# Cross-attention over 12544 keys: the keys' low part taken at another place in Vector's order

## The chip, the cores and the metric

The kernel runs on one core of a Trainium2 chip. The metric is the device time of one execution in microseconds; lower is better. The core has a matrix engine (TensorE, PE in the rows; PEld is its weight load), Vector (DVE), Scalar (ACT), GpSimd (POOL) and SyncE (SP), which here issues all transfers. Each engine works through its own list of instructions in order, and they meet only at semaphores.

## The reference

The reference is four layers on a state x of 128 rows and 256 columns. Each layer adds a cross-attention over a context of 12544 rows, then a self-attention, then a feed-forward block, each from a layer norm of x. The change touches the cross-attention of layers 0, 2 and 3. Layer 3's is, in short:

```python
q = _split_heads(query @ Wq + bq)          # 16 heads of 16
k = _split_heads(key @ Wk + bk)            # key = value = the context, 12544 x 256
v = _split_heads(value @ Wv + bv)
logits = jnp.einsum('bhqd,bhkd->bhqk', q, k) / jnp.sqrt(jnp.float32(DH))
logits = logits + mask * -1000000000.0
attn = jax.nn.softmax(logits, axis=-1)
out = jnp.einsum('bhqk,bhkd->bhqd', attn, v)
return out @ Wo + bo
```

Layer 0 has a mask and no Wo, layer 2 no mask.

## The kernel before, in words

`cross_attention_turned` (called for the stages L0x, L2x and L3x) goes through the keys in 14 blocks of 896 (`NB`, `KB2`), with a running maximum per query and head. A block has 16 waves; a wave g handles two heads and one half of the block (448 keys for the maxima). Every operand of an exact product is split into a high part, rounded to the matrix engine's format, and a low part, the difference.

In each wave PE makes two maximum products (L904, `maxima`), each into one of three banks `m_bank`; Vector reduces each to one column of `tops` (L1132, `top_of`) and so frees the bank. The product at place n of the ring waits for the one at place n - 3: the second product of wave g + 1 waits for the first maximum of wave g, and the first product of wave g + 2 for the second maximum of wave g. Seven waves later (`LAG`) PE makes the scores of the same wave (L915, `scores`), Scalar takes their exponentials (L1037), and every other wave PE multiplies them with the values (L940).

After four waves a group of heads has its maxima. At g % 4 == 0 Vector takes the highest of the three columns (L1146, `raise_top`) and splits it into two columns of `nat`: a cast (L1156) and a subtract (L1158), `split_top`. In wave g + 1 PE turns these (L927, `turn_q`), after it has waited for the split, and Scalar copies the result into `q_sub`.

Beside this the next block is projected. In the odd waves PE runs `project_next`: items 0 to 3 in waves 1, 3, 5 and 7 are the keys (L877), items 4 to 7 in waves 9 to 15 the values (L882). All items share one bank, `p_proj`. For a key item Scalar writes the high part with the bias (L1021, `evacuate`) and Vector the low part (L1093, `k_low`), in the even wave that follows: item i in wave 2i + 2. The next item waits on PE until the bank has been read (`k_split` counts the low parts):

```python
if i <= 4:
    e.wait_ge(sem("k_split"), 4 * b + i)
```

PE's order in a wave is maxima, scores, values, project_next, turn_q.

SyncE waits for the fourth low part of a block, then issues 24 transfers that stack the keys (L763), and behind them the load of the context for the block after next (L745). POOL (`split_ctx`) waits for that load, casts it (L833) and subtracts (L835) into `ctx_part`. It then works on the running maximum and scales the accumulator once a block (L854, after Scalar has made alpha in wave 4).

Vector's order in a wave, written out by hand at L1168 to L1182, was: first maximum, raise, second maximum, split, accumulate, k_low.

Of the kernel before, what the change touches and what calls it, by code (L numbers as in the profile page):

```python
# [23 lines left out]
class Module:  # L24
# [8 lines left out]
    def ps(self, name, shape=(P, 512), dtype=F32):  # L33
        return self.stack.enter_context(self.nc.psum_tensor(f"{self.name}_{name}", list(shape), dtype))

    def sem(self, name):

        if name not in self.sems:
            self.sems[name] = self.nc.alloc_semaphore(f"{self.name}_{name}")
        return self.sems[name]  # L40
# [597 lines left out]
NB = NKEYS // KB2  # L638
QUADS = 4
SLOTS = 8  # L640
WAVES = 16
# [9 lines left out]
def cross_attention_turned(nc, st, name, w, mask_kind):  # L651
# [53 lines left out]
    p_proj, p_oT = ps("p_proj"), ps("p_oT")  # L705
# [7 lines left out]
    def m_at(g, i):  # L713
        k = g % WAVES
        return g // WAVES * M_BLOCK + 2 * k + i + (k > 11)
    m_o_at = lambda b: (b + 1) * M_BLOCK + M_O
    def m_done(n):
        return (n + 1 - (n >= M_O) if n < NB * M_BLOCK else NB * M_BLOCK - (n < NB * M_BLOCK + M_O))
# [14 lines left out]
    with nc.Block() as block:  # L733

        @block.sync
        def _(e):
# [10 lines left out]
            def stack(b):  # L747
                odd = b % 2

                if b >= 2:  # L750
                    e.wait_ge(sem("s_made"), s_done(s_at((b - 2) * WAVES + 15, 1)))
                if mask_kind:
                    for r in range(2):
                        at = GROUP * r + MASK
                        e.dma_start(k_stack[at:at + 2, odd].bitcast(F32),
                                    mask_dram[:, b * KB2:(b + 1) * KB2].bitcast(F32).unsqueeze(1).broadcast_to([2, SLOTS, KB2])
                                    ).then_inc(sem(f"mask_stacked_{odd}"), 16)
                e.wait_ge(sem("k_split"), b * 4 + 4)
                for j in range(QUADS):
                    for r in range(2):  # L760
                        for n, (_, part) in enumerate(PRODUCTS):
                            at, of = GROUP * r + HD * n, HD * (2 * j + r)
                            e.dma_start(k_stack[at:at + HD, odd, j::4, :].bitcast(F32),  # L763
                                        kT[of:of + HD, odd, part].bitcast(F32)).then_inc(sem(f"k_stacked_{odd}_{j}"), 16)
# [323 lines left out]
        def _(e):  # L1088

            def k_low(b, i, bank):  # L1090
                part, keys = i // 2, slice(i % 2 * HALF, (i % 2 + 1) * HALF)
                e.wait_ge(sem("k_high"), 4 * b + i + 1)
                e.scalar_tensor_tensor(kT[:, b % 2, LOW, part, keys], bank[:, 0:HALF], bias_k[:, part:part + 1],  # L1093
                                       kT[:, b % 2, HIGH, part, keys].bitcast(F32), ALU.add, ALU.subtract).then_inc(sem("k_split"), 1)
# [33 lines left out]
            def top_of(g, r):  # L1128
                b, half = g // WAVES, g % 4 // 2
                n, h = m_at(g, r), g // 4 % 4 * 4 + g % 2 * 2 + r  # L1130
                e.wait_ge(sem("m_made"), m_done(n))
                e.tensor_reduce(tops[:, b % 2, h, half:half + 1], m_bank[n % RING][:, 0:HALF], AX,  # L1132
                                ALU.max).then_inc(sem("m_free"), 1)
# [3 lines left out]
            def raise_top(q):  # L1137
                b, h = q // 4, q % 4 * 4
                e.wait_ge(sem("m_free"), m_done(m_at(4 * q + 3, 1)))
                if b:  # L1140
                    e.wait_ge(sem("kept"), b)
                else:
                    e.wait_ge(sem("tops_set"), 1)
                if b >= 2:
                    e.wait_ge(sem("stepped"), b - 1)
                e.tensor_reduce(top[:, b % 2, h:h + 4], tops[:, b % 2, h:h + 4, :], AX, ALU.max).then_inc(sem("raised"), 1)  # L1146

            def split_top(q):
                b, h = q // 4, q % 4 * 4
                t = top[:, b % 2, h:h + 4].rearrange("q (p r) -> q p r", p=2)  # L1150
                if b:
                    e.wait_ge(sem("s_made"), s_done(s_q_at(q - 4)))
                else:
                    e.wait_ge(sem("q_max_made"), 2)
                e.wait_ge(sem("raised"), 3 * q + 1)
                e.tensor_copy(columns(q, HIGH).bitcast(F32R), t).then_inc(sem("raised"), 1)  # L1156
                e.wait_ge(sem("raised"), 3 * q + 2)
                e.tensor_tensor(columns(q, LOW).bitcast(F32R), t, columns(q, HIGH), ALU.subtract).then_inc(sem("raised"), 1)  # L1158

            def accumulate(b):  # L1160
                n = m_o_at(b)
                e.wait_ge(sem("m_made"), m_done(n))
                e.wait_ge(sem("scaled"), b + 1)
                a = acc[:, :, 0:HD + 1]
                e.tensor_tensor(a, a, m_bank[n % RING][:].rearrange("p (h d) -> p h d", h=HX)[:, :, 0:HD + 1],
                                ALU.add).then_inc(sem("m_free"), 1)

            for g in range(LAST_G):  # L1168
                u = g - LAG
                if g < WAVE_END:  # L1170
                    top_of(g, 0)
                if g % 4 == 0 and 0 < g <= WAVE_END:
                    raise_top(g // 4 - 1)
                if g < WAVE_END:
                    top_of(g, 1)
                if g % 4 == 0 and 0 < g <= WAVE_END:
                    split_top(g // 4 - 1)
                if u % WAVES == 4 and u > 4:
                    accumulate(u // WAVES - 1)

                if g % 2 == 0 and g // WAVES + 1 < NB and 0 < g % WAVES <= 8:
                    k_low(g // WAVES + 1, g % WAVES // 2 - 1, p_proj)  # L1182

            e.wait_ge(sem("m_free"), m_done(m_o_at(NB - 1)))
            e.reciprocal(rsum[:], acc[:, :, HD]).then_inc(sem("rsum"), 1)
# [1373 lines left out]
```

## Time and profile before

| | us |
|---|---|
| three runs, median (lowest to highest) | 2619.21 (2602.45 to 2624.37) |
| the profiled execution | 2617.17 |
| its span, first to last instruction | 2615.4 |
| L0x, L2x, L3x, blocks 1 to 12 together | 1213.35 |
| mean granted TensorE clock | 0.914 |

The span is that of the profiled execution; around it lie 1.8 us. In the rows, a start is counted from the span's first instruction, and a block starts with its first maximum product. The profile has one more large stage, L1x (another function), and the small layers between.

### The profile page before, as it was taken

How to read it: one execution, taken by the hardware profiler on the slowest of the kernel's cores; microseconds unless marked ns; L12 is line 12 of the kernel's file. 1: busy time of each engine (PE TensorE's matmuls, PEld its weight loads, DVE VectorE, ACT ScalarE, POOL GpSimd, SP SyncE). 2: the span in 40 equal slices, each digit the busy share in tenths (PEclk: the TensorE clock that was granted, in tenths of full speed). 3: DMA queues.
4: the chain of work that ended last, by engine and by line, in shares of the span. 5: the costliest groups of instructions: out<-in, count | busy, mean ns of one | idle time of the engine just before them, and what ended most of it. 6: DMA issues, size and time to landing. Idle time of an engine off the chain costs nothing. (4 is left out here: it accounts for less than half of the span.)

```text
span 2615.4 us, 67791 instructions
## 1 busy us (share of the span) xinstructions
PE 2300.0 (88%) x26351; PEld 1866.4 (71%) x26351; DVE 1703.0 (65%) x4076; ACT 1482.2 (57%) x2965; POOL 405.9 (16%) x345
## 2 busy tenths in 40 slices
PE   6999999877999999996666999999955999999958
PEld 4788888675777777775535778877743888788738
DVE  4666666527888888886724666676725666666632
ACT  2666666625777777774023666666621666666621
POOL 3221112002211221210001122222001122222000
PEclk7999999989999999997577899999956899999959
DMA  5666666365444344332044766666514666666525
GB/s 119 111 116 118 117 118 104 47 208 148 108 120 105 99 117 120 94 83 55 1 134 80 121 113 107 112 107 107 77 46 91 123 112 113 110 114 116 74 82 201
DMA packets 149181, 277.48 MB, mean 106 GB/s; under 512 B 31599, under 2 KB 69312, under 8 KB 148941
## 3 DMA queue, kind: packets, MB, share of 16 engines
q1 hardware_dynamic: 148942, 274.13, 51.2%
q8 instruction: 171, 2.80, 0.4%
q14 instruction: 68, 0.56, 0.1%
HBM read 118.86 MB, written 0.33 MB: 46 GB/s over the span
## 5 line engine op out<-in xcount | busy, mean ns | idle before, releaser
L1132 DVE TENSOR_REDUCE L3x_tops<-L3x_m_bank 128x1 f32<-128x448 f32 x448 | 262.0, 619 | 156.8 <-PE L3x_m_bank L904 154.8
L1132 DVE TENSOR_REDUCE L0x_tops<-L0x_m_bank 128x1 f32<-128x448 f32 x448 | 262.0, 619 | 154.8 <-PE L0x_m_bank L904 152.7
L1132 DVE TENSOR_REDUCE L2x_tops<-L2x_m_bank 128x1 f32<-128x448 f32 x448 | 262.0, 619 | 148.8 <-PE L2x_m_bank L904 146.7
L454 ACT ACTIVATE L1x_prob<-L1x_p_s,L1x_neg_max 128x512 f32<-128x512 f32 (+1 forms) x400 | 275.8, 689 | 117.8 <-DVE L1x_neg_max L565 115.1
L560 DVE CUSTOM_DVE_ANT_0 L1x_p_s<-L1x_p_s,L1x_mask 128x512 f32<-128x512 f32 (+1 forms) x400 | 273.7, 684 | 35.8 <-PE L1x_p_s L320 30.5
L1037 ACT ACTIVATE L2x_prob<-L2x_s_bank 128x512 f32<-128x512 f32 x448 | 219.5, 542 | 92.0 <-PE L2x_s_bank L915 90.8
L1037 ACT ACTIVATE L3x_prob<-L3x_s_bank 128x512 f32<-128x512 f32 x448 | 219.5, 542 | 91.9 <-PE L3x_s_bank L915 90.8
L1037 ACT ACTIVATE L0x_prob<-L0x_s_bank 128x512 f32<-128x512 f32 x448 | 219.5, 542 | 90.4 <-PE L0x_s_bank L915 89.2
L329 PE MATMUL L1x_p_t<-net_ident,L1x_prob 128*128 128x128 f32 x1568 | 239.0, 273 | 10.6 <-ACT L1x_probT L175 10.5
L329 PEld LDWEIGHTS L1x_p_t<-net_ident,L1x_prob 128*128 128x128 f32 x1568 | 192.1, 140 | 48.8 <-ACT L1x_probT L175 13.6
L320 PE MATMUL L1x_p_s<-L1x_k_stack,L1x_q_stack 96*128 96x512 f32 (+1 forms) x400 | 182.2, 457 | 1.9 <-DVE L1x_q_stack L544 1.9
L175 ACT COPY L1x_probT<-L1x_p_t 128x512 f32<-128x512 f32 (+1 forms) x300 | 173.1, 577 | 5.1 <-PE L1x_p_t L329 5.1
L915 PEld LDWEIGHTS L3x_s_bank<-L3x_q_sub,L3x_k_stack 52*128 52x128 f32 x1568 | 124.2, 191 | 9.8 <-ACT L3x_prob L1037 6.6
L915 PEld LDWEIGHTS L2x_s_bank<-L2x_q_sub,L2x_k_stack 50*128 50x128 f32 x1568 | 123.8, 190 | 9.6 <-ACT L2x_prob L1037 6.3
L915 PEld LDWEIGHTS L0x_s_bank<-L0x_q_sub,L0x_k_stack 52*128 52x128 f32 x1568 | 122.8, 189 | 9.4 <-ACT L0x_prob L1037 6.1
L346 PE MATMUL L1x_p_oT<-L1x_probT,L1x_v 128*32 128x128 f32 x3136 | 126.9, 279 | 0.5 <-ACT L1x_probT L175 0.5
L915 PE MATMUL L3x_s_bank<-L3x_q_sub,L3x_k_stack 52*128 52x128 f32 x1568 | 116.9, 262 | 3.1 <-ACT L3x_prob L1037 2.9
L915 PE MATMUL L2x_s_bank<-L2x_q_sub,L2x_k_stack 50*128 50x128 f32 x1568 | 116.7, 262 | 3.1 <-ACT L2x_prob L1037 2.9
L904 PE MATMUL L0x_m_bank<-L0x_k_stack,L0x_q_max 52*128 52x448 f32 x448 | 111.9, 479 | 8.2 <-DMA L0x_k_stack<-L0x_kT 6.7
L904 PE MATMUL L3x_m_bank<-L3x_k_stack,L3x_q_max 52*128 52x448 f32 x448 | 112.2, 481 | 7.9 <-DMA L3x_k_stack<-L3x_kT 6.4
L915 PE MATMUL L0x_s_bank<-L0x_q_sub,L0x_k_stack 52*128 52x128 f32 x1568 | 115.5, 260 | 3.1 <-ACT L0x_prob L1037 2.9
L904 PE MATMUL L2x_m_bank<-L2x_k_stack,L2x_q_max 50*128 50x448 f32 x448 | 110.4, 476 | 4.4 <-DMA L2x_k_stack<-L2x_kT 2.5
(724 smaller groups left out, 4524.0 us busy)
## 6 DMA issues: line engine op xcount, KB each, us to landing
L0x_k_stack<-L0x_kT SPq DMA_DIRECT2D x336, 112.0 KB, 4.0
L2x_k_stack<-L2x_kT SPq DMA_DIRECT2D x336, 112.0 KB, 4.0
L3x_k_stack<-L3x_kT SPq DMA_DIRECT2D x336, 112.0 KB, 4.0
L1x_k_stack<-L1x_kT SPq DMA_DIRECT2D x288, 128.0 KB, 2.4
L3f_w<-in_L_ffn_w SPq DMA_DIRECT2D x16, 1024.0 KB, 9.2
L0x_ctx<-in_ctxT SPq DMA_DIRECT2D x14, 896.0 KB
L2x_ctx<-in_ctxT SPq DMA_DIRECT2D x14, 896.0 KB
L3x_ctx<-in_ctxT SPq DMA_DIRECT2D x14, 896.0 KB
```

The costliest lines, as they stand in the source:

```text
L175: copy(probT[:, h % PT_RING, 0:nk], p_t[h % T_RING][:, 0:nk]).then_inc(sem(copied(h)), 1)
L320: e.matmul(p_s[h % S_RING][:, 0:nk], q_stack[0:ROWS, h, :], k_stack[0:ROWS, odd, h // 2, 0:nk], start=True, stop=True).then_inc(sem("score ...
L329: i = e.transpose(p_t[h % T_RING][:, t * P:(t + 1) * P], prob[:, h % P_RING, t * P:(t + 1) * P], ident[:])
L346: i = e.matmul(p_oT[VW * s:VW * s + VW, g * P:(g + 1) * P], v[:, odd, t, h, :], probT[:, h % PT_RING, t * P:(t + 1) * P], start=t == 0, st ...
L454: e.activation(prob[:, h % P_RING, 0:nk], p_s[h % S_RING][:, 0:nk], ACT.Exp, bias=neg_max[:, odd, h:h + 1]).then_inc(sem("exped"), 1)
L560: e.tensor_tensor_reduce(s, s, mask[:, odd, 0:nk], 1.0, -3e38, ALU.add, ALU.max, block_max[:, h:h + 1]).then_inc(sem("head_maxed"), 1)
L904: e.matmul(m_bank[n % RING][:, 0:HALF], q_max[rows_of(r), slot_of(g), :], k_stack[rows_of(r), b % 2, slot_of(g), half * HALF:(half + 1) * ...
L915: mm = e.matmul(s_bank[s_at(u, r) % RING][:, at * P:(at + 1) * P], k_stack[rows_of(r), b % 2, slot_of(u), t * P:(t + 1) * P], q_sub[rows_o ...
L1037: e.activation(prob[:, k % 3, u % 2 * 2 + r, 0:nt, :].rearrange("p t n -> p (t n)"), s_bank[n % RING][:, 0:nt * P], ACT.Exp).then_inc(sem( ...
L1132: e.tensor_reduce(tops[:, b % 2, h, half:half + 1], m_bank[n % RING][:, 0:HALF], AX, ALU.max).then_inc(sem("m_free"), 1)
```

## The change

In Vector's loop the low part is taken directly behind the first maximum of an even wave. Before, it came last in the wave. The waits and counts of all instructions are the same.

```diff
                 if g < WAVE_END:
                     top_of(g, 0)
+
+                if g % 2 == 0 and g // WAVES + 1 < NB and 0 < g % WAVES <= 8:
+                    k_low(g // WAVES + 1, g % WAVES // 2 - 1, p_proj)
                 if g % 4 == 0 and 0 < g <= WAVE_END:
                     raise_top(g // 4 - 1)
                 if g < WAVE_END:
...
                     split_top(g // 4 - 1)
                 if u % WAVES == 4 and u > 4:
                     accumulate(u // WAVES - 1)
-
-                if g % 2 == 0 and g // WAVES + 1 < NB and 0 < g % WAVES <= 8:
-                    k_low(g // WAVES + 1, g % WAVES // 2 - 1, p_proj)
```

So the order becomes: first maximum, k_low, raise, second maximum, split. In waves 2 and 6 there is no raise and no split; in waves 4 and 8 there are both.

## Rows read from the trace of the kernel before

**Rows 1.** The page, part 1: busy time, share of the span, instructions.

```profile
PE 2300.0 (88%) x26351; PEld 1866.4 (71%) x26351; DVE 1703.0 (65%) x4076; ACT 1482.2 (57%) x2965; POOL 405.9 (16%) x345
```

**Rows 2.** Windows: blocks 1 to 12 of L0x, L2x, L3x; columns in the first line.

```profile
core 0: us, PE busy (x) PEld busy (x) DVE busy (x) ACT busy (x) POOL busy (x), PEclk, DMA share, GB/s
75.12:478.58 403.46, 387.71 (x5354) 325.95 (x5353) 274.29 (x588) 262.97 (x553) 75.25 (x58) 0.99 0.65 112
1465.29:1870.85 405.56, 387.66 (x5354) 325.70 (x5353) 276.42 (x588) 262.98 (x553) 75.19 (x58) 0.99 0.64 108
2052.40:2456.73 404.33, 388.97 (x5354) 327.32 (x5353) 273.91 (x588) 262.97 (x553) 75.27 (x58) 0.98 0.65 112
```

**Rows 3.** PE's waits in L0x, all blocks: us in total, times, longest.

```profile
PE L0x_p_proj L882 <- DVE L0x_kT L1093: 15.9, 13, 4.0
PE L0x_p_proj L877 <- DVE L0x_kT L1093: 5.2, 15, 0.7
```

**Rows 4.** Windows of three single blocks of L0x, columns as in rows 2.

```profile
280.01:312.60 32.59, 31.94 (x448) 26.85 (x447) 22.19 (x49) 21.92 (x47) 6.75 (x5) 1.00 0.64 111
176.49:212.30 35.81, 33.47 (x448) 28.18 (x447) 23.88 (x49) 21.91 (x47) 6.73 (x5) 0.95 0.69 116
345.70:379.45 33.75, 31.95 (x447) 26.85 (x446) 23.34 (x49) 21.92 (x47) 6.74 (x5) 1.00 0.65 115
```

**Rows 5.** Timeline of PE, block from 280.01: start, us, instruction [idle before <-releaser].

```profile
290.50 1.48 PE L877 MATMUL L0x_p_proj<-L0x_ctx_part,L0x_wk_part 128*128 128x448 f32 x6 [0.32 <-DVE L0x_kT L1093]
...
297.65 0.47 PE L904 MATMUL L0x_m_bank<-L0x_k_stack,L0x_q_max 52*128 52x448 f32 x2
...
298.73 1.70 PE L882 MATMUL L0x_p_proj<-L0x_wv_part,L0x_ctx_part 128*128 128x256 f32 x12 [0.33 <-DVE L0x_kT L1093]
300.27 0.38 PE L927 MATMUL L0x_s_bank<-net_ident,L0x_nat 128*128 128x128 f32 x2
300.58 0.47 PE L904 MATMUL L0x_m_bank<-L0x_k_stack,L0x_q_max 52*128 52x448 f32 x2
...
306.67 0.47 PE L904 MATMUL L0x_m_bank<-L0x_k_stack,L0x_q_max 52*128 52x448 f32 x2
...
309.20 0.48 PE L904 MATMUL L0x_m_bank<-L0x_k_stack,L0x_q_max 52*128 52x448 f32 x2
```

**Rows 6.** Timelines of Vector and Scalar, waves 6 to 9 of that block.

```profile
293.72 0.68 DVE L1093 SCALAR_TENSOR_TENSOR L0x_kT<-L0x_p_proj,L0x_bias_k,L0x_kT 128x448 fp32r<-128x448 f32 x1
...
296.57 0.62 DVE L1132 TENSOR_REDUCE L0x_tops<-L0x_m_bank 128x1 f32<-128x448 f32 x1 [1.07 <-PE L0x_m_bank L904]
...
297.71 0.17 DVE L1156 CAST L0x_nat<-L0x_top 128x4 fp32r<-128x4 f32 x1
...
298.00 0.68 DVE L1093 SCALAR_TENSOR_TENSOR L0x_kT<-L0x_p_proj,L0x_bias_k,L0x_kT 128x448 fp32r<-128x448 f32 x1
298.59 1.15 DVE L1132 TENSOR_REDUCE L0x_tops<-L0x_m_bank 128x1 f32<-128x448 f32 x2
...
296.18 0.63 ACT L1021 ACTIVATE L0x_kT<-L0x_p_proj,L0x_bias_k 128x448 fp32r<-128x448 f32 x1 [0.35 <-PE L0x_p_proj L877]
```

**Rows 7.** Timeline of POOL: the split's subtract L835, the scaling L854.

```profile
89.44 4.03 POOL L835 TENSOR_TENSOR L0x_ctx_part<-L0x_ctx,L0x_ctx_part 128x1792 fp32r<-128x1792 f32 x1
...
254.84 0.66 POOL L854 TENSOR_TENSOR L0x_acc<-L0x_acc,L0x_alpha 128x272 f32<-128x272 f32 x1 [7.54 <-ACT L0x_alpha L1049]
...
292.93 4.03 POOL L835 TENSOR_TENSOR L0x_ctx_part<-L0x_ctx,L0x_ctx_part 128x1792 fp32r<-128x1792 f32 x1
...
2405.36 4.03 POOL L835 TENSOR_TENSOR L3x_ctx_part<-L3x_ctx,L3x_ctx_part 128x1792 fp32r<-128x1792 f32 x1
```

**Rows 8.** Timeline of Vector: casts and low parts of other blocks.

```profile
58.95 0.68 DVE L1093 SCALAR_TENSOR_TENSOR L0x_kT<-L0x_p_proj,L0x_bias_k,L0x_kT 128x448 fp32r<-128x448 f32 x1
...
92.78 0.71 DVE L1156 CAST L0x_nat<-L0x_top 128x4 fp32r<-128x4 f32 x1
...
253.18 0.62 DVE L1132 TENSOR_REDUCE L0x_tops<-L0x_m_bank 128x1 f32<-128x448 f32 x1 [1.08 <-PE L0x_m_bank L904]
...
2376.62 0.68 DVE L1093 SCALAR_TENSOR_TENSOR L3x_kT<-L3x_p_proj,L3x_bias_k,L3x_kT 128x448 fp32r<-128x448 f32 x1
```

## Prediction, made before the changed kernel was run

> **What bounds the kernel now.** I read the page first, then the windows of the stages, the waits on TensorE (PE), single blocks, and the timeline of the waves that the change touches. The page has PE busy for 88% of the span [rows 1]. The change sits in the function that stages L0x, L2x and L3x call; blocks 1 to 12 of them fill 1213.35 us, 36 blocks of 33.70 us on average, with PE busy 96% of that and its granted clock at 0.98 to 0.99 [rows 2]. PE sets the pace. What PE waits for is nearly always k_low (L1093 on Vector, DVE): in L0x 15.9 us ahead of the value projection L882 and 5.2 us ahead of the key projection L877 [rows 3].
>
> These waits are of two kinds. The short one is in every block. In wave 5 PE stands 0.32 us for k_low before L877, in wave 9 0.33 us before L882; wave 9 lasts 300.58 - 297.65 = 2.93 us, while wave 13, with the same work and no k_low, lasts 309.20 - 306.67 = 2.53 [rows 5]. So the wait costs 0.40 a wave, and this block of 32.59 us is otherwise without a gap worth naming: PE is busy for 31.94 of it [rows 4].
>
> The long one comes from GpSimd (POOL). The split's cast L1156 takes 0.17 us when undisturbed [rows 6], but in one block it starts at 92.78, in the middle of POOL's subtract L835 (89.44 to 93.47), and ends at 93.49 [rows 7, 8]. In block 0 k_low starts only at 58.95 for that reason, and PE waits 4.0 us [rows 3, 8]. Whenever the cast of wave 8 meets L835, it stands until L835 is over, and k_low stands behind it in Vector's queue, with PE waiting. Two stretched blocks show the price: one lasts 33.75 at full clock, the other 35.81 at clock 0.95 with PE busy 33.47 instead of 31.94, 1.53 us more for the same work [rows 4]. Over the 36 blocks the excess above the undisturbed 32.59 is 1213.35 - 36 x 32.59 = 40.1 us.
>
> **The change, step by step.** Nothing is added or taken away; four k_low a block move ahead, in waves 2 and 6 past one maximum (0.61 us), in waves 4 and 8 past raise, maximum, cast and subtract as well. No wait value changes.
>
> *What goes from PE.* In wave 8 the first maximum starts at 296.57 and is over by 297.19; k_low starts now at 298.00 [rows 6], then at about 297.13, and ends at 297.81 instead of 298.68. PE could begin L882 0.40 earlier than 298.73, at 298.33 [rows 5], so k_low is there 0.5 in advance and the whole 0.40 goes. The same holds for wave 4 with wave 5. In waves 2 and 6 PE doesn't wait for k_low, so that move brings nothing: 0. Saved: 2 x 0.40 x 36 = 29 us. An undisturbed block then lasts 31.79.
>
> *Does k_low then wait itself?* It needs ScalarE's high part, L1021, which ends at 296.18 + 0.63 = 296.81, 0.38 before the first maximum ends [rows 6]. Cost 0; both come from the same PE stream, so an earlier projection moves both.
>
> *What the second maximum's delay costs.* It frees its bank some 0.7 us later (about 298.4, or 298.0 once wave 5's saving is counted). The next to use that bank is the first maximum product of wave 10, at 300.58 - 0.80 = 299.78 [rows 5]. Cost 0, with 1.7 us in hand. Vector's total for the wave is the same, so wave 9's maxima start where they do now (298.59 [rows 6]).
>
> *The collision with L835.* It doesn't go: the cast now starts about 0.55 us behind the end of k_low. SyncE issues the next stack of keys behind k_low of wave 8, then the context load, and POOL's cast and subtract follow the load. From that k_low's end to the end of the next L835 it takes X: 93.47 - 59.63 = 33.84 us in the first case, 2409.39 - 2377.30 = 32.09 in the last of 33 [rows 7, 8]; over all 33 the least is 31.7, the mean 32.9, the most 34.3. The cast is then held for X - 31.79 - 0.55, some 0.6 us on average and 2.0 at most. What is behind it now? Not k_low, but PE's transpose L927 (it wants the split) and wave 9's maxima. L927 comes at 300.27 - 0.80 = 299.47 [rows 5], behind a projection that PE can do meanwhile, and the split would be ready near 298.3: 1.15 us of cover. The first maximum of wave 9 would end near 298.9, wanted at 299.9: about 0.95 us of cover. Held times above 0.95 occur in 8 of the 33 cases and sum to 3.2 us for 36 blocks; with 1.53 us for a lower clock once, 5 us remain of the 40. The ends of this cost are 0 (all covered) and 36 x 0.6 = 22 us, if nothing is covered; I take 5, since a 1.5 us projection is queued ahead of L927.
>
> *A second meeting.* In wave 4 the cast moves by 0.6 us, to about 254.95 (the first maximum starts at 253.18 [rows 8]), and there it meets POOL's L854, 254.84 to 255.50 [rows 7]. It would be held 0.55 us in each block. The maxima of wave 5 then end 0.3 us before they are wanted. Cost 0; uncovered it would be 36 x 0.55 = 20 us.
>
> *Is k_low itself held by POOL?* k_low of wave 6 starts at 293.72 and takes 0.68 us, inside an L835 that runs from 292.93 to 296.96 [rows 6, 7]. So it isn't, and it needs no cover. The Trainium skill says otherwise for some forms ("SBUF — State Buffer", section "SBUF: two separate sides"): one pair of ports is an exclusive lock between GpSimd and a Vector instruction that runs in a two-port mode or has two SBUF inputs, for the whole instruction. k_low reads keys and a bias column from SBUF beside its bank; counted as two, it would stand behind L835 like the cast. The trace decides against that count, and agrees with the rule on the cast.
>
> *Block 0.* PE waits more there: in L0x 5.2 - 12 x 0.32 = 1.4 us before L877 and 4.0 before L882 [rows 3], where L927 still comes behind the held cast, so that about the projection's 1.7 to 2.5 us are won. That makes about 4 us in L0x; I put 2 each on L2x and L3x, whose waits were shorter. 8 us, between 3 and 12.
>
> *SyncE and the stack.* k_low of wave 8 ends 1.3 us earlier, 0.4 of it from wave 5; the 24 issues start earlier with it, and their data is wanted one block on. Nothing waits for them now in blocks 1 to 12, and nothing will. 0.
>
> **The sum.** 2617.17 (the profiled execution, span 2615.4) - 29 - (40 - 5) - 8 = 2545 us. The median of the runs shown is 2619.21, 2 us above the profiled one, within their spread of 22 us; I keep 2545.
>
> **Rivals.**
> 1. *Less cover.* The held cast (0.6 a block), wave 5's lateness and clock losses reach PE after all, because L927 or the maxima turn out to be wanted earlier. For: the cover of wave 5 is only 0.3 us. Against: in a wave PE always has scores and a projection between. 22 us instead of 5, and 5 for wave 5: 2567.
> 2. *k_low is held by POOL* at its new place, with a later phase of L835. Then the long waits stay and only wave 5's 0.40 x 36 = 14 us go, with 3 in block 0: 2600. Against: the 0.68 us above. The lock rule of the Trainium skill's SBUF page is the one that would bring it about.
> 3. *The change doesn't do what it says*, since the ring of k_low, stack, load and L835 sets the block's length anyway. For: X is 32.9, close to the mean block of 33.70. Against: blocks of 32.59 exist. Time: 2617.
> 4. *Slower: a collision in every block.* Now a stretched block often puts the next one out of L835's way. With k_low ahead of the cast that relief is gone, and the cast meets L835 nearly always. It costs more than before only if X grows, with the transfers crowded into shorter blocks: at X + 1.5 us the cast is held 2.1, 1.15 beyond the cover, and with 1.53 for the clock the block lasts 31.79 + 1.15 + 1.53 = 34.5 against 33.70: + 28 - 8, 2637. It decides from about X + 0.9 on. Against: over the 33 cases X is no larger behind the short blocks than behind the long ones.
>
> **How the numbers follow.** Forecast 2545 with a chance of 0.69, its own range 2528 to 2562 (block 0, the remainder, the spread of the runs). Rival 1 0.18, rival 2 0.05, rival 3 0.03, rival 4 0.05. A measurement of this kernel can tell about 1%, 26 us: below 2591 lie the forecast and rival 1, 0.87; within it rivals 2 and 3, 0.08; above it rival 4, 0.05. The range takes in rival 1 with what is unknown of it and stops before rival 2: 2525 to 2590.
>
> **What would show it.** PE's waits for k_low gone in blocks 1 to 12, wave 9 at 2.53 us where nothing collides; casts of wave 8 held for 0 to 2 us in most blocks, casts of wave 4 at about 0.7 us; blocks of 31.8 us; clock 1.00 through the stages; L1093 still at 0.68. Wrong if L927 or L904 takes over the waits, if L1093 shows long ones, or if the blocks stay above 32.5.

## The result, and the profile after

Five runs of the changed kernel have a median of 2536.29 us (2535.30 to 2556.27), beside 2619.21 for the kernel before. The ratio is 0.9708, with a 95% interval of 0.9657 to 0.9758; it is worked out from all runs, not from the two medians, whose quotient is 0.9683. The profiled execution is the slowest of the five, 2556.27 us; the other four lie between 2535.30 and 2539.48. Compared execution with execution, the profiled one is 2617.17 - 2556.27 = 60.9 us shorter than the profiled one of before.

Blocks 1 to 12 of the three stages, which answer to [rows 2], columns as there:

```profile
73.92:457.30 383.38, 382.47 (x5353) 322.57 (x5352) 275.94 (x588) 263.24 (x553) 75.26 (x58) 1.00 0.67 116
1450.09:1833.65 383.56, 382.90 (x5355) 322.93 (x5354) 279.70 (x588) 263.26 (x553) 75.39 (x58) 1.00 0.68 115
2016.74:2398.70 381.96, 381.96 (x5353) 322.42 (x5352) 274.92 (x588) 263.02 (x553) 75.34 (x58) 1.00 0.69 118
```

They sum to 1148.90 us, 64.4 less than 1213.35. PE is busy for all but 1.6 of them, and its clock stays at 1.00. 25 of the 36 blocks last 31.79 us. A second trace of the changed kernel, taken later, has 1156.15 us in them:

```profile
73.48:456.70 383.22, 382.25 (x5353) 322.38 (x5352) 277.01 (x588) 263.25 (x553) 75.30 (x58) 1.00 0.68 116
1455.30:1841.71 386.41, 383.53 (x5354) 323.12 (x5354) 282.80 (x588) 263.47 (x553) 75.29 (x58) 1.00 0.66 111
2017.83:2404.35 386.52, 385.76 (x5355) 325.14 (x5354) 276.85 (x588) 262.94 (x552) 75.29 (x58) 0.99 0.68 116
```

The rest of this section reads the first trace. The waits of PE in L0x, which answer to [rows 3], no longer name k_low at all:

```profile
PE L0x_m_bank L904 <- DMA L0x_k_stack<-L0x_kT: 6.4, 1, 6.4
PE L0x_s_bank L927 <- DVE L0x_nat L1158: 3.2, 3, 2.3
PE L0x_m_bank L904 <- DVE L0x_tops L1132: 1.5, 4, 0.5
```

PE's timeline around wave 9 of the block from 266.55 answers to [rows 5], the one of Vector behind it to [rows 6]; the last fence has POOL's subtract of that block:

```profile
283.79 0.47 PE L904 MATMUL L0x_m_bank<-L0x_k_stack,L0x_q_max 52*128 52x448 f32 x2
...
284.47 1.70 PE L882 MATMUL L0x_p_proj<-L0x_wv_part,L0x_ctx_part 128*128 128x256 f32 x12
286.00 0.38 PE L927 MATMUL L0x_s_bank<-net_ident,L0x_nat 128*128 128x128 f32 x2
286.31 0.47 PE L904 MATMUL L0x_m_bank<-L0x_k_stack,L0x_q_max 52*128 52x448 f32 x2
```

```profile
282.71 0.62 DVE L1132 TENSOR_REDUCE L0x_tops<-L0x_m_bank 128x1 f32<-128x448 f32 x1 [1.07 <-PE L0x_m_bank L904]
283.25 0.68 DVE L1093 SCALAR_TENSOR_TENSOR L0x_kT<-L0x_p_proj,L0x_bias_k,L0x_kT 128x448 fp32r<-128x448 f32 x1
283.84 0.15 DVE L1146 TENSOR_REDUCE L0x_top<-L0x_tops 128x4 f32<-128x12 f32 x1
283.91 0.61 DVE L1132 TENSOR_REDUCE L0x_tops<-L0x_m_bank 128x1 f32<-128x448 f32 x1
284.44 0.50 DVE L1156 CAST L0x_nat<-L0x_top 128x4 fp32r<-128x4 f32 x1
```

```profile
280.88 4.03 POOL L835 TENSOR_TENSOR L0x_ctx_part<-L0x_ctx,L0x_ctx_part 128x1792 fp32r<-128x1792 f32 x1
```

The projection starts 0.68 us behind the maximum products, and the wave lasts 286.31 - 283.79 = 2.52 us. The cast is still held until L835 ends at 284.91, for 0.34 us here. But k_low has gone ahead of it, undisturbed inside L835, and L927 comes only at 286.00.

### The profile page after: what moved, and what is told of

Read it like the earlier page. It is cut to its first block and busy times, and to the rows that moved or that the text cites. A ratio compares the mean times of both kernels' runs of the same rounds, so it can differ in the third digit from the quotient of the medians.

```text
span 2554.4 us, 67791 instructions
## 1 busy us (share of the span) xinstructions
PE 2292.1 (90%) x26351; PEld 1858.9 (73%) x26351; DVE 1709.9 (67%) x4076; ACT 1483.3 (58%) x2965; POOL 406.1 (16%) x345
```

## The experiments

Times are medians; each ratio is against the kernel before, run beside it on the same chip. The runs were spread over three chips, on which the kernel before had medians of 2618.96, 2619.99 and 2619.89. "Blocks" are blocks 1 to 12 of the three stages, 36 in all, from the profiled execution.

**GpSimd kept off the cast, in both orders.** Both kernels put one wait ahead of POOL's split of the context:

```diff
                 if b + 2 < NB:
+                    e.wait_ge(sem("raised"), 12 * b + 6)
                     split_ctx(b + 2)
```

In the old order:

> Order of before; GpSimd's context split (L833, L835) waits until the maxima of waves 0 to 7 are split, so it can't meet the cast of wave 8. If the long waits come from that meeting: the cast of wave 8 takes 0.17 us in every block, blocks 1 to 12 last 32.59 us each (1173 in all against 1213), the short waits of 0.32 us stay, time 2619 - 40 - 4 = 2575, between 2565 and 2585. Rival, that k_low's place in Vector's order makes the long waits and GpSimd only happens to run then: blocks stay at 33.7 on average, 2619.

Measured: 2572.59 us, ratio 0.9810 (0.9774 to 0.9846). The windows, the casts of the whole stage (here on L1157: duration least/median/most in ns) and PE's waits in L0x:

```profile
73.83:464.73 390.90, 383.19 (x5353) 322.15 (x5352) 266.03 (x588) 262.83 (x553) 75.12 (x58) 1.00 0.67 116
1460.30:1851.22 390.92, 383.21 (x5353) 322.13 (x5352) 266.02 (x588) 262.82 (x553) 75.13 (x58) 1.00 0.66 112
2032.67:2423.56 390.89, 383.18 (x5353) 322.12 (x5352) 266.02 (x588) 262.82 (x553) 75.12 (x58) 1.00 0.68 116
```

```profile
L1157 DVE CAST L0x_nat<-L0x_top x56: 158/160/172, 46.1 to 490.3; 128x4 fp32r<-128x4 f32 x56
```

```profile
PE L0x_p_proj L878 <- DVE L0x_kT L1094: 5.0, 14, 0.7
PE L0x_p_proj L883 <- DVE L0x_kT L1094: 3.9, 12, 0.3
```

No cast is held any more, the blocks last 32.55 to 32.59 us, and of PE's waits for k_low only the short ones are left in them. k_low's place was the same as before, so its place alone doesn't make the long waits: without the meeting with POOL there are none. That settles it against the rival. The windows also divide the price of the meeting, 1213.35 - 1172.71 = 40.6 us: PE stood still for 49.0 us before [rows 2] and for 23.1 here, 25.9 less. The other 14.8 are busy time, 1164.34 against 1149.58: ten of the 36 blocks of before had a mean clock of 0.95, and here none is below 1.00.

In the new order:

> Order of after, with the same wait on GpSimd. Theory: what the changed kernel still loses to the meeting (1148.9 - 36 x 31.79 = 4.5 us in blocks 1 to 12, and casts of 3.5 and 3.3 us in block 0 of L0x and L3x) goes; every block 31.79, time about 2528, 8 below the changed kernel's 2536. Rival: GpSimd's later split holds back the next context load and the projection that needs it, then blocks get longer than 31.79 and nothing is gained or it is slower than 2536.

Measured: 2528.23, ratio 0.9656 (0.9626 to 0.9686), blocks of 1144.52 in all, with PE busy in every microsecond of them:

```profile
68.30:449.81 381.51, 381.51 (x5353) 322.08 (x5352) 271.36 (x588) 263.02 (x553) 75.29 (x58) 1.00 0.71 119
1436.71:1818.21 381.50, 381.50 (x5353) 322.10 (x5353) 271.37 (x588) 263.01 (x553) 75.30 (x58) 1.00 0.69 115
```

Both were run once more side by side, unchanged:

> The changed kernel with GpSimd's wait, unchanged from its first run, for a direct comparison with the changed kernel: 6 to 10 us below it (4.5 of the blocks 1 to 12, the rest from block 0). Rival, that its lead was one chip against another: no difference.

> The changed kernel once more, beside the others on one chip: 2536 within 8.

Measured on that chip: 2533.01, ratio 0.9653 (0.9615 to 0.9690), against 2535.64 and 0.9686 (0.9649 to 0.9723). The lead of 3 us, where 6 to 10 were expected, lies inside both intervals. In the traces the blocks are shorter, 1148.45 and 1144.52 against 1156.15 and 1148.90; 3.9 of the 1148.45 are one block at clock 0.88, with PE busy all through it. That this kernel beats the changed one in device time is likely but not shown.

**One place at a time.** Here k_low is put at the new place only in some of its waves, and stays at the old in the others:

```diff
+                if g % WAVES in (8,):
+                    low_next(g)
                 if g % 4 == 0 and 0 < g <= WAVE_END:
                     raise_top(g // 4 - 1)
...
-                if g % 2 == 0 and g // WAVES + 1 < NB and 0 < g % WAVES <= 8:
-                    k_low(g // WAVES + 1, g % WAVES // 2 - 1, p_proj)
+                if g % WAVES in (2, 4, 6):
+                    low_next(g)
```

`low_next(g)` is the same k_low under a short name. The other three kernels have (4,), (2, 6) and (4, 8) at the new place.

> Only the k_low of wave 8 is at the new place, those of waves 2, 4 and 6 at the old one. Theory of two parts: it frees wave 9's 0.40 us and takes k_low out from behind the held cast; an undisturbed block lasts 32.19, blocks 1 to 12 about 1164 with 5 us left of the collision, time 2619 - 49 - 6 = 2564. Rival, that all the gain lies in wave 8: 2536. Rival, that the collision is what counts little: 2605.

> Only the k_low of wave 4 is at the new place. Theory: 36 x 0.40 = 14 us go, k_low of wave 8 still stands behind the held cast, so the long waits stay; time about 2604, between 2595 and 2612. Rival, that the order in wave 4 sets where GpSimd's split falls and so the collisions: below 2590.

> Only the k_low of waves 2 and 6 are at the new place. Theory: PE doesn't wait for them, nothing changes, 2619 within 8. Rival, that each of the four moves brings its part: 2600 or less.

> The k_low of waves 4 and 8 at the new place, those of 2 and 6 at the old. Theory: equal to the changed kernel, blocks of 31.79 where nothing collides, 2536 within 8. Rival, that the early k_low of waves 2 and 6 is needed to keep Vector ahead: blocks above 31.9.

| k_low moved in | us | ratio (95%) | blocks, sum |
|---|---|---|---|
| wave 8 | 2562.06 | 0.9769 (0.9729 to 0.9809) | 1162.42 |
| wave 4 | 2614.89 | 0.9986 (0.9960 to 1.0011) | 1216.41 |
| waves 2 and 6 | 2616.07 | 1.0001 (0.9976 to 1.0026) | 1210.30 |
| waves 4 and 8 | 2537.74 | 0.9665 (0.9614 to 0.9716) | 1147.22 |

Wave 8 alone gives 57 us by the medians, as expected, and waves 2 and 6 give nothing. Waves 4 and 8 are the whole change. Wave 4 alone missed its 14 us: it gave nothing that can be measured, yet on top of wave 8 it is worth 2562.06 - 2537.74 = 24 us by the medians and 15.2 us in the blocks. The windows of wave 4 alone, and its longest subtract L1158 in L0x:

```profile
74.10:478.91 404.81, 390.20 (x5353) 328.26 (x5353) 283.98 (x588) 263.15 (x553) 75.03 (x58) 0.98 0.65 112
1466.10:1873.58 407.48, 390.62 (x5355) 329.03 (x5354) 284.40 (x588) 262.82 (x553) 75.07 (x58) 0.97 0.64 107
2050.74:2454.86 404.12, 388.25 (x5353) 326.80 (x5353) 284.07 (x588) 262.91 (x553) 75.15 (x58) 0.98 0.66 112
```

```profile
L1158 DVE TENSOR_TENSOR L0x_nat<-L0x_top,L0x_nat x56: 166/167/1682, 47.0 to 504.7; 128x4 fp32r<-128x4 f32 x56
```

The undisturbed blocks of this kernel do last 32.19 us instead of 32.59. But 36 of them save 14.4 us, and the blocks came out 3.1 longer than before, so 17.5 us were lost elsewhere. The trace has about 16 of them: the casts of wave 8 are held for 32.6 us in all, against 25.9 in the trace of before; in four blocks L1158 of wave 4 takes 1.58 to 1.68 us, which makes each about 1.2 us longer (the section on the longer meeting shows how); and PE is busy for 4.7 us more at the lower clock. One more kernel takes the meeting away and moves wave 4 alone:

> GpSimd's wait and only the k_low of wave 4 at the new place. Moving that one alone gave 5 us instead of 14. Theory: a shorter block lets the held cast start earlier against GpSimd's subtract, which follows the last k_low at a fixed distance, so the wait in wave 8 grows by what wave 5 saves; with the meeting gone the whole 0.40 us a block is kept: blocks of 32.19, time 2572.6 - 14.4 = 2558. Rival, that the move in wave 4 costs something itself (its cast then meets L854): blocks above 32.3, time 2565 or more.

Measured: 2550.79, ratio 0.9732 (0.9686 to 0.9778); all blocks 32.19:

```profile
73.01:459.32 386.31, 382.45 (x5353) 322.19 (x5353) 271.38 (x588) 262.81 (x553) 75.15 (x58) 1.00 0.69 116
1445.57:1831.88 386.31, 382.45 (x5353) 322.19 (x5352) 271.38 (x588) 262.80 (x553) 75.15 (x58) 1.00 0.67 113
```

Against the 1172.71 of the old order with the wait, the blocks sum to 1158.91: 13.8 us are kept once nothing gives them back (the medians say 22, more than the blocks).

**Ahead of the split, but behind the second maximum.**

```diff
                     top_of(g, 1)
+                if g % 2 == 0 and g // WAVES + 1 < NB and 0 < g % WAVES <= 8:
+                    k_low(g // WAVES + 1, g % WAVES // 2 - 1, p_proj)
                 if g % 4 == 0 and 0 < g <= WAVE_END:
                     split_top(g // 4 - 1)
...
-                if g % 2 == 0 and g // WAVES + 1 < NB and 0 < g % WAVES <= 8:
-                    k_low(g // WAVES + 1, g % WAVES // 2 - 1, p_proj)
```

> k_low stands behind the second maximum but ahead of the split. Theory: the collision is off k_low, and most of the short wait goes too (k_low ends at about 298.4 where PE could take it at 298.3): undisturbed blocks of 31.9 to 32.1; the cast starts 0.15 us later than in the changed kernel, the cover is the same. Time 2545 to 2565. If the place ahead of the second maximum is what counts, the short waits stay at 0.32 us and it is 2565 or more; if only the place ahead of the split counts, it equals the changed kernel, 2536.

Measured: 2566.46, ratio 0.9798 (0.9761 to 0.9835), just above the expected range; most blocks last 31.98 to 32.03, as expected, and the 36 sum to 1159.75. In the blocks, passing the split is what counts most: it brings all but 11 us of the 64. The last 0.24 us of a block need the place ahead of the second maximum. The medians are further apart than that, 2566 against 2536, while the two profiled executions differ by 11 like the blocks. Where the other 19 us between the medians lie isn't known, since of the changed kernel only executions 20 us and more above its median were traced.

**What POOL holds.**

```diff
-                e.tensor_copy(columns(q, HIGH).bitcast(F32R), t).then_inc(sem("raised"), 1)
+                e.tensor_reduce(columns(q, HIGH).bitcast(F32R), tops[:, b % 2, h:h + 4].rearrange("q (p r) n -> q p r n", p=2),
+                                AX, ALU.max).then_inc(sem("raised"), 1)
```

> Order of before; the high part of the split is made by a maximum over the three columns (a reduce, like L1146, which ran undisturbed inside L835) instead of the cast. Theory, by the lock rule's second clause: the reduce isn't held, but the subtract L1158 behind it reads two tensors of SBUF and L835 reads SBUF too, so L1158 is held in its place, as once in block 0 of L2x (1.53 us): the long waits stay, 2619 within 8. Rival, that only copies in a two-port mode are held: L1158 stays at 0.17 us, the long waits go, 2575.

Measured: 2614.10, ratio 0.9987 (0.9961 to 1.0013). The reduce in the cast's place, and the subtract behind it (L1159 here):

```profile
L1156 DVE TENSOR_REDUCE L3x_nat<-L3x_tops x56: 154/157/168, 2016.6 to 2475.3; 128x4 fp32r<-128x12 f32 x56
```

```profile
L1159 DVE TENSOR_TENSOR L0x_nat<-L0x_top,L0x_nat x56: 166/168/2304, 46.3 to 503.2; 128x4 fp32r<-128x4 f32 x56
L1159 DVE TENSOR_TENSOR L3x_nat<-L3x_top,L3x_nat x56: 166/167/3928, 2016.8 to 2475.5; 128x4 fp32r<-128x4 f32 x56
```

The reduce is never held; the subtract takes over the whole wait. By the Trainium skill ("SBUF — State Buffer", section "SBUF: two separate sides") GpSimd's instruction holds a Vector instruction that runs in a two-port mode, and one with two SBUF inputs if GpSimd's reads SBUF. The traces agree: the cast within SBUF was held (up to 3.60 us in the trace of before), and so was the subtract with its two SBUF inputs (up to 3.93 us here). That the cast ran in a two-port mode no row shows.

**A longer meeting.**

```diff
+                e.tensor_tensor(ctx_part[:, odd, LOW, 0], ctx[:, 0], ctx_part[:, odd, HIGH, 0].bitcast(F32),
+                                ALU.subtract).then_inc(sem("ctx_half"), 1)
+                e.wait_ge(sem("ctx_half"), b)
                 e.tensor_tensor(ctx_part[:, odd, LOW], ctx[:], ctx_part[:, odd, HIGH].bitcast(F32),
                                 ALU.subtract).then_inc(sem("ctx_split"), 1)
```

> Order of after; GpSimd makes half of the subtract once more ahead of L835 (same values), some 2.1 us, so the meeting ends that much later. Theory: the cast of wave 8 is held up to 2.1 us longer, beyond the cover of 0.92 us; a late block makes the next meeting shorter, so on average (35.0 - 31.79 - 1.47) / 2 = 0.87 us of lateness a block: blocks of 32.7, plus up to 0.5 each for a lower clock; time 2565 to 2590. Rival, that the meeting is always covered in the new order: 2536.

Measured: 2598.46, ratio 0.9906 (0.9871 to 0.9942), blocks of 1219.02 in all, 33.86 on average. The direction is right and the size is not: blocks came out 0.7 us beyond the top of what was expected, and the time 8 us. The cast of wave 8 takes 2.9 to 3.9 us in twelve blocks, every second one of blocks 1 to 8 of each stage. Of the 2.07 us by which a block is longer than 31.79 on average, 0.79 are PE's busy time at a lower clock, in seven blocks (mean clock 0.79 to 0.95), where the expectation had up to 0.5. Another 0.31 come from ten blocks in which the cast of wave 8 isn't held and which still last 32.9, because of a meeting in wave 4 that the expectation left out. The rest, 0.97, is near the 0.87 expected. The first trace of the changed kernel has the meeting in wave 4 once, in block 1 of L0x, here by Vector, POOL and PE:

```profile
83.98 0.60 DVE L1156 CAST L0x_nat<-L0x_top 128x4 fp32r<-128x4 f32 x1
84.62 1.58 DVE L1158 TENSOR_TENSOR L0x_nat<-L0x_top,L0x_nat 128x4 fp32r<-128x4 f32 x1
```

```profile
83.90 0.66 POOL L854 TENSOR_TENSOR L0x_acc<-L0x_acc,L0x_alpha 128x272 f32<-128x272 f32 x1 [7.53 <-ACT L0x_alpha L1049]
84.50 1.68 POOL L833 CAST L0x_ctx_part<-L0x_ctx 128x1792 fp32r<-128x1792 f32 x1
```

```profile
86.26 0.44 PE L927 MATMUL L0x_s_bank<-net_ident,L0x_nat 128*128 128x128 f32 x2 [0.75 <-DVE L0x_nat L1158]
```

Where the context has landed by the time POOL scales the accumulator, L833 follows at once. L854 holds the cast, and L833 then holds the subtract until both end at 86.2, 1.4 us beyond its usual 0.17, which is more than PE has in hand: it waits 0.75 us.

## Why the prediction was right

*The short waits: right to the hundredth.* An undisturbed block was put at 31.79 us and lasts 31.79; 36 of them make the 29 us. Moving k_low in waves 2 and 6 was put at nothing and brought nothing.

*The collision: right, with its cover.* The cover is how long a cast can be held before PE runs out of other work. The meeting was to remain, at X - 31.79 - 0.55, and to be hidden up to 0.95 us. The casts of wave 8 were held for 0.44 us on average over the 36 blocks and 1.79 at most, where 0.6 and 2.0 had been put (0.53 and 2.35 in the second trace). In 28 blocks of three kernels of the new order (the changed one twice, and waves 4 and 8) a cast was held 0.90 us or more. In each, what it was held less what the block was longer than 31.79 comes to 0.90 to 0.94. One of them is the block from 234.21, where the cast takes 1.62 us:

```profile
252.11 1.62 DVE L1156 CAST L0x_nat<-L0x_top 128x4 fp32r<-128x4 f32 x1
```

```profile
234.21:266.55 32.34, 32.18 (x448) 27.05 (x447) 23.98 (x49) 22.04 (x47) 6.77 (x5) 1.00 0.74 123
```

It is held 1.62 - 0.16 = 1.46, the block is 32.34 - 31.79 = 0.55 longer: 0.91 are covered. The cover of L927 alone was put higher, at 1.15 us, and that came true as well:

```profile
252.14 1.69 PE L882 MATMUL L0x_p_proj<-L0x_wv_part,L0x_ctx_part 128*128 128x256 f32 x12
253.99 0.44 PE L927 MATMUL L0x_s_bank<-net_ident,L0x_nat 128*128 128x128 f32 x2 [0.16 <-DVE L0x_nat L1158]
```

L927 comes 1.85 us behind the start of L882, where it came 1.53 behind in the block from 266.55; 0.32 of the 1.46 reach it, and 1.14 are covered.

What was left over of the collision was put at 5 us and measures 1148.90 - 36 x 31.79 = 4.5. That the sum is so near is partly luck. Its first term, held times beyond the cover, was put at 3.2 and measures 3.3. Its second, 1.53 for a lower clock once, did not occur in this trace; 1.1 for the second meeting came instead. In the second trace of the changed kernel the same remainder is 1156.15 - 1144.44 = 11.7 us: 4.7 beyond the cover in wave 8, 3.4 for three second meetings, and 3.6 for one block 1 at clock 0.89.

*k_low isn't held.* Its new place in wave 8 begins inside an L835 in 31 blocks, and there it takes 0.67 to 0.68 us each time, no longer than elsewhere.

*The second meeting.* The cast of wave 4 takes 0.61 us in 36 blocks of 36, as forecast (0.7), and it is covered. Not foreseen was that L833 can follow L854 without a pause. That cost 1.1 us once in the first trace and in block 1 of all three stages in the second.

*Block 0* was put at 8 us. It shrank from 41.17 to 38.98, from 37.30 to 33.52 and from 39.11 to 38.04: 7.0 together. This agreement shows little. L0x gave 2.2 of its 4, and in the second trace the three last 38.95, 43.93 and 34.94, which is 117.8 us, against 117.6 in the kernel before.

*The sum.* 29 + 35 + 8 = 72 us were forecast. The three stages, each from the first to the last instruction on its tiles, went from 516.1, 514.6 and 520.1 us to 492.7, 491.5 and 495.6, that is 71; in the second trace they last 494.2, 502.2 and 499.6, and the difference is 55. In the first trace the profiled executions differ by only 61, since the rest of the program, which the change doesn't touch, took 10 us longer (L1f 70.3 against 64.1, L1x 627.1 against 623.0). The four other runs lie 20 us lower and were not traced; the median, 2536, is 9 us under the 2545, and what makes up these 9 stays open. In the second trace of the changed kernel one block 0 lasted 43.93 us at clock 0.61, where the first trace has 33.51 at 0.80. Such blocks, at the start of a stage, are one source of that spread; that they are all of it wasn't tried.

The rivals: less cover (2567) fell with the 0.92 us, k_low held by POOL (2600) with L1093's durations. The ring of k_low, stack, load and L835 (2617) fell as a rival for the changed kernel, but the runs showed a part of it at work in the old order, which the prediction had not used. There a block that gets 0.4 us shorter reaches its cast 0.4 us earlier, while L835 follows the last k_low at its distance X. In the kernel with wave 4 alone the casts of wave 8 were held 6.7 us longer in all, which gives back nearly half of the 14.4; the four meetings in wave 4 and the lower clock gave back most of the rest. The share of each is read from one trace. Tested was only that the whole loss goes when POOL's split is kept off both waves, by the kernel that waits. So the 29 may be counted in full only once k_low is out from behind the cast: the two parts of the change don't add up one by one.

## What to carry to other kernels

When a wait's length varies from block to block, look for an instruction that took far longer than its median, and at what GpSimd was doing until the moment it ended; then put whatever the critical engine waits for ahead of that instruction in Vector's queue. The collision itself may stay, if its length is less than the work that the critical engine has in hand. A saving ahead of such a collision can be given back there, as the 14 us of wave 4 were, so take the collision off the critical engine's path first and shorten the block second.

## What was not expected of the hardware

Two GpSimd instructions back to back held two Vector instructions in a row: L854 the cast, until 84.58, and L833 the subtract, until 86.20, with L833 getting in between. And the length of PE's wait didn't decide whether a block kept its clock. In the kernel before, one block had a mean clock of 0.95 with a wait of 1.42 us, another 1.00 with a wait of 1.98:

```profile
244.84:280.01 35.17, 33.43 (x447) 28.05 (x446) 23.29 (x49) 21.91 (x47) 6.75 (x5) 0.95 0.68 117
1735.20:1769.44 34.24, 31.94 (x447) 26.84 (x446) 23.84 (x49) 21.91 (x47) 6.73 (x5) 1.00 0.64 108
```

```profile
264.66 2.18 PE L882 MATMUL L0x_p_proj<-L0x_wv_part,L0x_ctx_part 128*128 128x256 f32 x12 [1.42 <-DVE L0x_kT L1093]
1755.58 1.70 PE L882 MATMUL L2x_p_proj<-L2x_wv_part,L2x_ctx_part 128*128 128x256 f32 x12 [1.98 <-DVE L2x_kT L1093]
```

In the two traces of the changed kernel one block of the 72 shows less than 1.00: block 1 of L3x in the second, at 0.89. The same block had 0.88 in a kernel that waits, with PE busy throughout, so the meeting isn't needed for that.
